# Low-rank feed-forward stage: the inner product in fp32r over split factors, and the order of the work around it

## The chip, the cores and the metric

One Trainium2 chip, one of its cores. The metric is the device time of one execution in microseconds; each version's number is the median of several executions. Smaller is better.

## What is computed

The reference is a network of eight stages over x (4 x 1024 rows of 256, fp32), in the order A M B M C F D F. Stages A and C are attentions, M is an expert feed-forward, B a retention, D a gated recurrence. This case is about F, which runs twice with the same weights, as stage 5 and as stage 7 (the last):

```python
def _L1_ffn_ref(x, U1, V1, b1, U2, V2, b2):
    D_MODEL, D_FF, RANK = (256, 1024, 64)
    P = jnp.einsum('bsd,dr->bsr', x, U1)
    H = jax.nn.gelu(jnp.einsum('bsr,rf->bsf', P, V1) + b1)
    Q = jnp.einsum('bsf,fr->bsr', H, U2)
    return jnp.einsum('bsr,rd->bsd', Q, V2) + b2
...
x = x + _L1_ffn_ref(_layernorm(x, axis=-1), L1_ffn_U1, ...)
```

So a row of 256 is normalised, brought down to 64 numbers, up to 1024 with a gelu, down to 64 and up to 256 again, and added to x.

## The kernel before, in words

X, all 4096 rows, stays in SBUF for the whole network. `low_rank_ffn` (L158) takes it in NG = 8 groups of 512 rows, each of them four tiles of 128. Every engine has its own program, in which the order of the work is written out by hand; the engines meet through semaphores that start at START = 4 and are waited for with constants or loop values.

What one group takes:

- **Row normalisation**, class `LayerNorm` (L70). VectorE takes four moments (L104, L107), GpSimd adds epsilon (L119) and raises to the power -1/2 (L123), VectorE scales the rows into `ln_h` (L113). There is one buffer of `ln_h`, so the rows of the next group wait until TensorE has transposed those of this one (L111). TensorE turns them over into `ps_t` (`tensor`, L125), ScalarE copies them to `hT` (`scalar`, L134).
- **first** (L273): U1 on the normalised rows. The 256 features are two halves; each half makes a product of 64 rows, the two of them side by side in the array's columns 0 to 63 and 64 to 127 (`tile_position`), so `ps_p` has two partial sums of P stacked on 128 partitions. ScalarE copies them to `PT` (L249).
- **hidden** (L281), the inner product: eight matmuls, m = 0 to 7, of V1 stacked twice (128 x 128) on `PT` (128 x 512) in fp32, which adds the two partial sums on the way. Their results go through two banks, `ps_h` (L179), to ScalarE's gelu (L255). The profile shows an fp32 matmul as two records.
- **down** (L286): U2, two matmuls of 64 columns side by side, into `ps_q`; ScalarE copies it to `QT` (L259).
- **out** (L311): V2 on `QT`, four matmuls of 256 columns into the two banks of `ps_o`; VectorE adds them to X (L239). GpSimd has added the bias b2 to the same rows of X before that (L223), once their normalisation was read.

The turns are skewed (`skewed_turns`, L147, a loop of three rounds with two turns each, and two turns behind it): in turn g the engines do the normalisation of group g + 2 besides. On VectorE it stands ahead of the two adds of group g (L234 to L240), on GpSimd ahead of the bias of group g (L219 to L224), on TensorE ahead of the last down. TensorE's order in a turn is: eight hidden matmuls with three downs between them, the transposes of g + 2, the last down, first of g + 1, and then the four of out, which wait for the copy `QT`.

The weights come in eight DMAs on SyncE's queue (L144). TensorE and ScalarE wait for all of them. The next stage begins when all engines have passed a barrier. In stage 7 SyncE also stores each group of X when its adds are done (L205).

Of the kernel before, what the change touches and what calls it, by code (L numbers as in the profile page):

```python
# [13 lines left out]
ds = bass.ds  # L14
# [143 lines left out]
def low_rank_ffn(nc, ph, X, ident, U1, V1, b1, U2, V2, b2, out=None):  # L158

    R, FF = U1.shape[1], V1.shape[1]
    M = FF // P
    hT = ph.sb("hT", [P, 2, DC, GT])
    u1 = ph.sb("u1", [P, DC, R])
    v1 = ph.sb("v1", [P, FF])  # L170
    bias1 = ph.sb("bias1", [P, M])
# [23 lines left out]
    with nc.Block() as block:  # L195
# [14 lines left out]
        def _(pool):  # L210
            ln.pool_setup()
            pool.wait_ge(ln.rs, START + 1)
            ln.pool(pool, 0)
            ln.pool(pool, 1)
            pool.wait_ge(weights, loaded)

            def turn(g, h, following, more):
                if more:
                    ln.pool(pool, g + 2)  # L219
                x4 = X[:, ds(g * G, G), :]  # L220
                pool.wait_ge(ln.hrow, START + (g + 1) * G)
                pool.sem_inc(passed, 1)
                nc.gpsimd.tensor_tensor(x4, x4, bias2[:, :].unsqueeze(1).to_broadcast([P, G, D]),  # L223
                                        ALU.add).then_inc(b_add, 1)  # L224
            skewed_turns(pool, turn)

        @block.vector
        def _(dve):
            ln.vector(dve, 0)
            ln.vector(dve, 1)  # L230

            def turn(g, h, following, more):
                if more:
                    ln.vector(dve, g + 2)  # L234
                dve.wait_ge(b_add, START + g + 1)
                for k in range(G // 2):
                    dve.wait_ge(o_mm, START + g * (G // 2) + k + 1)
                    x2 = X[:, ds(g * G + 2 * k, 2), :]
                    nc.vector.tensor_tensor(x2, ps_o[:, k, :].rearrange("p (j d) -> p j d", j=2), x2,  # L239
                                            ALU.add).then_inc(o_add, 1)  # L240
            skewed_turns(dve, turn)

        @block.scalar
        def _(act):
            act.wait_ge(weights, loaded)

            def first(g):
                act.wait_ge(p_mm, START + g + 1)
                nc.scalar.copy(PT[:, :], ps_p[:, :]).then_inc(p_sb, 1)  # L249

            def turn(g, h, following, more):
                act.wait_ge(q_mm, START + g)
                for m in range(M):
# [2062 lines left out]
```

## Time and profile before

| | us |
|---|---|
| median of 3 executions | 3752.79 (3745.21 to 3757.0) |
| the profiled execution, its own time | 3747.93 |
| its span, first to last instruction | 3746.0 |
| stage 7: weights landed to last add | 3610.35 to 3741.73 |

The profile is one execution. Engines: PE is TensorE's matmuls and PEld its weight loads, DVE is VectorE, ACT ScalarE, POOL GpSimd, SPq SyncE's queue. Times in a view are microseconds from the start of the span, except the mean of one instruction, which is in nanoseconds. Tiles carry the stage in their name: `s5F_` and `s7F_` are the two stages of this case. "<-" behind a tile name means made from; in square brackets stands how long the engine sat idle before, and what ended that. Granted clock 1.00 is TensorE at 2.4 GHz, 0.50 at 1.2 GHz.

### The profile page before, as it was taken

What the parts mean: (1) busy time and instruction counts of PE and PEld (TensorE: products, weight loads), DVE (VectorE), ACT (ScalarE), POOL (GpSimd) and SP (SyncE); (2) the same over time, 40 slices, a digit from 0 to 9 for tenths busy, and PEclk for the clock granted to TensorE, in tenths of its full rate; (3) what the DMA queues carried; (4) which work ended last, traced back from release to release, by engine and by line L of the source; (5) the groups of instructions that cost most, each with busy time, mean ns of one, the idle gap of its engine ahead of it and who ended that gap; (6) DMA issues with size and microseconds to landing.
All of it is one profiled execution on the core that took longest, in us unless ns stands there. A gap on an engine that the chain in (4) does not pass through costs nothing. (4 is left out here: it accounts for less than half of the span.)

```text
span 3746.0 us, 71603 instructions
## 1 busy us (share of the span) xinstructions
PE 3177.9 (85%) x21448; PEld 2163.5 (58%) x21448; DVE 2350.6 (63%) x5285; ACT 2075.7 (55%) x3467; POOL 854.2 (23%) x1660
## 2 busy tenths in 40 slices
PE   6699999999999639997883599959688888797879
PEld 3366666666666429996452499944355555533433
DVE  4488888888886564444557544435477777435853
ACT  3589898989897214443111344422267676354544
POOL 2211111111110114553001245523422222120112
PEclk9799999999999869998896799979899999898879
DMA  3300000000000314433003244331211111000001
GB/s 116 101 23 25 25 24 23 25 25 23 23 25 16 113 51 90 90 79 74 11 0 113 70 91 90 72 82 57 86 52 52 51 51 50 24 0 12 0 18 39
DMA packets 148660, 186.78 MB, mean 50 GB/s; under 512 B 20304, under 2 KB 114768, under 8 KB 148560
## 3 DMA queue, kind: packets, MB, share of 16 engines
q1 hardware_dynamic: 123984, 151.94, 12.6%
q0 software_dynamic: 24576, 33.57, 5.5%
q8 instruction: 55, 0.90, 0.1%
q14 instruction: 45, 0.37, 0.0%
HBM read 122.54 MB, written 62.91 MB: 50 GB/s over the span
## 5 line engine op out<-in xcount | busy, mean ns | idle before, releaser
L1741 DVE CUSTOM_DVE_ANT_0 s0Ah_SD<-s0Ah_ps_s,s0Ah_table 128x1024 f32<-128x1024 f32 x512 | 622.9, 1217 | 40.6 <-PE s0Ah_ps_s L1832 25.3
L1787 ACT ACTIVATE s0Ah_PM<-s0Ah_SD,s0Ah_nb 128x1024 f32<-128x1024 f32 x512 | 594.6, 1161 | 24.8 <-POOL s0Ah_nb L1730 24.8
L1842 PEld LDWEIGHTS s0Ah_ps_t<-top_ident,s0Ah_PM 128*128 128x128 f32 x4096 | 480.6, 141 | 103.1 <-ACT s0Ah_PM L1787 3.4
L1842 PE MATMUL s0Ah_ps_t<-top_ident,s0Ah_PM 128*128 128x128 f32 x4096 | 533.6, 273 | 0.4
L1793 ACT COPY s0Ah_PT<-s0Ah_ps_t 128x512 f32<-128x512 f32 x512 | 302.9, 592 | 104.3 <-PE s0Ah_ps_t L1842 99.8
L1832 PE MATMUL s0Ah_ps_s<-s0Ah_ks,s0Ah_qs 96*128 96x512 bf16 x1024 | 308.5, 383 | 28.4 <-DMA s0Ah_ks<-s0A_parts 27.7
L2045 ACT ACTIVATE s4Ch_PM<-s4Ch_SD,s4Ch_nb 128x260 f32<-128x260 f32 (+2 forms) x512 | 254.3, 497 | 141.1 <-POOL s4Ch_nb L1988 128.1
L1749 DVE COPY s0Ah_PT<-s0Ah_ps_t 128x512 f32<-128x512 f32 x384 | 264.8, 690 | 94.5 <-PE s0Ah_ps_t L1842 91.7
L1730 POOL TENSOR_TENSOR s0Ah_nb<-s0Ah_mx,s0Ah_minus 128x1 f32<-128x1 f32 x512 | 98.2, 192 | 930.8 <-DVE s0Ah_mx L1741 930.8
L1855 PE MATMUL s0Ah_ps_v<-s0Ah_PT,s0Ah_Vs 128*32 128x512 f32 x2048 | 274.2, 608 | 0.0
L1999 DVE CUSTOM_DVE_ANT_0 s4Ch_SD<-s4Ch_ps_s,s4Ch_table 128x260 f32<-128x260 f32 (+2 forms) x512 | 204.6, 407 | 78.9 <-PE s4Ch_ps_s L2090 65.5
L2090 PE MATMUL s4Ch_ps_s<-s4Ch_ks,s4Ch_qs 96*128 96x256 bf16 (+2 forms) x896 | 142.4, 229 | 111.8 <-DMA s4Ch_ks<-s4C_parts 55.9
L1832 PEld LDWEIGHTS s0Ah_ps_s<-s0Ah_ks,s0Ah_qs 96*128 96x128 bf16 x1024 | 82.2, 117 | 243.0 <-issue 239.9
L2108 PE MATMUL s4Ch_ps_t<-top_ident,s4Ch_PM 128*128 128x128 f32 x960 | 196.3, 281 | 0.0
L1988 POOL TENSOR_TENSOR s4Ch_nb<-s4Ch_mx,s4Ch_minus 128x1 f32<-128x1 f32 x512 | 98.0, 191 | 376.7 <-DVE s4Ch_mx L1999 376.6
L1193 ACT ACTIVATE s3Me_hid<-s3Me_ps_h 128x512 f32<-128x512 f32 x128 | 76.7, 599 | 184.3 <-PE s3Me_ps_h L1231 184.3
L1193 ACT ACTIVATE s1Me_hid<-s1Me_ps_h 128x512 f32<-128x512 f32 x128 | 76.7, 599 | 183.2 <-PE s1Me_ps_h L1231 183.2
L2090 PEld LDWEIGHTS s4Ch_ps_s<-s4Ch_ks,s4Ch_qs 96*128 96x128 bf16 x896 | 70.9, 98 | 171.6 <-DVE s4Ch_mx L1999 123.9
L2008 DVE COPY s4Ch_PT<-s4Ch_ps_t 128x512 f32<-128x512 f32 x192 | 132.6, 691 | 35.3 <-PE s4Ch_ps_t L2108 34.2
L1148 DVE TENSOR_TENSOR s3Me_HT_rest<-s3Me_hid,s3Me_HT_top 128x512 fp32r<-128x512 f32 x128 | 89.0, 695 | 103.7 <-ACT s3Me_HT_top L1194 103.7
L1148 DVE TENSOR_TENSOR s1Me_HT_rest<-s1Me_hid,s1Me_HT_top 128x512 fp32r<-128x512 f32 x128 | 88.9, 695 | 102.9 <-ACT s1Me_HT_top L1194 102.9
L1094 POOL DMA_INDIRECT s3M_acc<-s3Me_ys,s3Me_keep x64 | 109.6, 1712 | 167.7 <-DVE s3Me_ys L1158 153.1
(391 smaller groups left out, 7414.3 us busy)
## 6 DMA issues: line engine op xcount, KB each, us to landing
s1M_raw_w<-in_L_ffn_w SPq DMA_DIRECT2D x16, 1024.0 KB, 5.5
s3M_raw_w<-in_L_ffn_w SPq DMA_DIRECT2D x16, 1024.0 KB, 5.8
s0A_parts<-s0Ap_sp SPq DMA_DIRECT2D x48, 256.0 KB, 2.4
s4C_parts<-s4Cp_sp SPq DMA_DIRECT2D x48, 256.0 KB, 2.4
s0Ah_qs<-s0A_parts SPq DMA_DIRECT2D x64, 96.0 KB
s0Ah_ks<-s0A_parts SPq DMA_DIRECT2D x64, 96.0 KB
s4Ch_qs<-s4C_parts SPq DMA_DIRECT2D x64, 96.0 KB
s4Ch_ks<-s4C_parts SPq DMA_DIRECT2D x64, 96.0 KB
```

The costliest lines, as they stand in the source:

```text
L1148: nc.vector.tensor_tensor(HT[1][:, m, :], hid[:, m % NH, :], HT[0][:, m, :].bitcast(F32), ALU.subtract).then_inc(h_rest, 1)
L1741: nc.vector.tensor_tensor_reduce(SD[u % NBUF][:, :], ps_s[u % 2][:, :, :].rearrange("p a n -> p (a n)"), table[:, (TB - 1 - t) * P:(TB - 1 ...
L1749: nc.vector.tensor_copy(PT[u // G % 2][:, 0:G, q:q + P], ps_t[:, 0, :].rearrange("p (k q) -> p k q", k=G)).then_inc(ta_ok, 1)
L1787: nc.scalar.activation(PM[u % NBUF][:, :], SD[u % NBUF][:, :], ACT.Exp, bias=nb[:, u:u + 1]).then_inc(e_ok, 1)
L1793: nc.scalar.copy(PT[u // G % 2][:, G:, q:q + P], ps_t[:, 1, :].rearrange("p (k q) -> p k q", k=G)).then_inc(tb_ok, 1)
L1832: x = nc.tensor.matmul(ps_s[u % 2][:, k, :], qs[s][:, t * P:(t + 1) * P], ks[s][:, k * GT:(k + 1) * GT], start=True, stop=True)
L1842: x = nc.tensor.transpose(ps_t[:, bank, k * P:(k + 1) * P], PM[u % NBUF][:, at:at + P], ident[:, :])
L1855: x = nc.tensor.matmul(ps_v[j * W:(j + 1) * W, :], Vs[v // 2][:, 2 * j + r, :], PT[v % 2][:, 2 * j + r, :], start=(r == 0), stop=(r == 1), ...
L1999: nc.vector.tensor_tensor_reduce(SD[u % NBUF][:, 0:n], ps_s[u % 2][:, 0:n], table[:, min(u % TB, 2), 0:n], HD ** -0.5, -3e38, ALU.add, ALU ...
L2045: nc.scalar.activation(PM[u % NBUF][:, 0:n], SD[u % NBUF][:, 0:n], ACT.Exp, bias=nb[:, u:u + 1]).then_inc(e_ok, 1)
L2090: x = nc.tensor.matmul(ps_s[u % 2][:, at:at + n], qs[s][:, t * P:(t + 1) * P], ks[s][:, k0:k0 + n], start=True, stop=True)
L2108: x = nc.tensor.transpose(bank[:, u % 2, k if t else 1, :], pm[:, k * P:(k + 1) * P], ident[:, :])
```

## The change

- `u1` is loaded twice side by side (one DMA more), and `first` is two full matmuls that accumulate in `ps_p`, so P stands whole on partitions 0 to 63 and again on 64 to 127.
- P and V1 are split into a top, which is the value rounded to fp32r, and a rest, the difference. ScalarE makes `v1_top` once and VectorE `v1_rest` once per stage. Per group ScalarE makes `PA` (top of P, all 128 partitions) and the upper half of `PB` (top again), VectorE the lower half of `PB` (rest of P, `rest_of`).
- `hidden` takes two m at a time: two fp32r matmuls of 128 rows (`v1_top` on `PB`, top and rest stacked), and two of 64 rows (`v1_rest` on `PA`, one on partitions 0 to 63, the other on 64 to 127). The product of the two rests is left out. One semaphore step for both.
- `ps_h` has four banks instead of two, `ps_t` and `ps_o` one instead of two.
- Normalisation runs three groups ahead instead of two, with two buffers of `ln_h`. The transposes of a group are two separate steps (`turned`).
- The out matmuls of group g move into group g + 1 (`outs`), the adds of group g on VectorE likewise (`added`); VectorE's order in a group is: adds of g - 1, `rest_of(g + 1)`, normalisation of g + 3.
- The loops are unrolled. Two semaphores more.

Lines that the change takes out of the vector, scalar and tensor programs are left out below; they stand in the printed kernel.

```diff
@@ -157,36 +157,36 @@
 
 def low_rank_ffn(nc, ph, X, ident, U1, V1, b1, U2, V2, b2, out=None):
 
     R, FF = U1.shape[1], V1.shape[1]
     M = FF // P
+    NH = 4
     hT = ph.sb("hT", [P, 2, DC, GT])
-    u1 = ph.sb("u1", [P, DC, R])
+    u1 = ph.sb("u1", [P, DC, P])
     v1 = ph.sb("v1", [P, FF])
+    v1_top, v1_rest = ph.sb("v1_top", [P, FF], F32R), ph.sb("v1_rest", [P, FF], F32R)
     bias1 = ph.sb("bias1", [P, M])
     u2 = ph.sb("u2", [P, M, R])
     v2 = ph.sb("v2", [P, D])
     bias2 = ph.sb("bias2", [P, D])
-    PT, QT = ph.sb("PT", [P, GT]), ph.sb("QT", [P, GT])
+    PA = [ph.sb(f"PA{i}", [P, GT], F32R) for i in range(2)]
+    PB = [ph.sb(f"PB{i}", [P, GT], F32R) for i in range(2)]
+    QT = ph.sb("QT", [P, GT])
     HT = ph.sb("HT", [P, M, GT])
-    ps_t = ph.ps("ps_t", [P, DC, GT])
+    ps_t = ph.ps("ps_t", [P, GT])
     ps_p = ph.ps("ps_p", [P, GT])
-    ps_h = ph.ps("ps_h", [P, 2, GT])
+    ps_h = ph.ps("ps_h", [P, NH, GT])
     ps_q = ph.ps("ps_q", [P, GT])
-    ps_o = ph.ps("ps_o", [P, 2, GT])
-    ln = LayerNorm(ph, X, ident, hT, ps_t)
+    ps_o = ph.ps("ps_o", [P, GT])
+    ln = LayerNorm(ph, X, ident, hT, None, buffers=2)
     weights, stored = ph.dma_sem("weights"), ph.dma_sem("stored")
-    p_mm, p_sb = ph.sem("p_mm"), ph.sem("p_sb")
+    vt_ok, vr_ok = ph.sem("vt_ok"), ph.sem("vr_ok")
+    p_mm, top_ok, rest_ok = ph.sem("p_mm"), ph.sem("top_ok"), ph.sem("rest_ok")
     h_mm, h_sb = ph.sem("h_mm"), ph.sem("h_sb")
     q_mm, q_sb = ph.sem("q_mm"), ph.sem("q_sb")
-    b_add, passed = ph.sem("b_add"), ph.sem("passed")
+    b_add = ph.sem("b_add")
     o_mm, o_add = ph.sem("o_mm"), ph.sem("o_add")
-    pairs = [(u1[:, :, :], U1.rearrange("(c p) r -> p c r", p=P)), (v1[0:R, :], V1), (v1[R:P, :], V1),
+    split_u1 = U1.rearrange("(c p) r -> p c r", p=P)
+    pairs = [(u1[:, :, 0:R], split_u1), (u1[:, :, R:P], split_u1), (v1[0:R, :], V1), (v1[R:P, :], V1),
              (bias1[:, :], b1.rearrange("(m p) -> p m", p=P)),
              (u2[:, :, :], U2.rearrange("(m p) r -> p m r", p=P)), (v2[0:R, :], V2), (v2[R:P, :], V2),
              (bias2[:, :], b2.rearrange("(a d) -> a d", a=1).to_broadcast([P, D]))]
@@ -210,111 +210,167 @@
         def _(pool):
             ln.pool_setup()
             pool.wait_ge(ln.rs, START + 1)
-            ln.pool(pool, 0)
-            ln.pool(pool, 1)
+            for g in range(3):
+                ln.pool(pool, g, g % 2)
             pool.wait_ge(weights, loaded)
-            def turn(g, h, following, more):
-                if more:
-                    ln.pool(pool, g + 2)
-                x4 = X[:, ds(g * G, G), :]
+            for g in range(NG):
+                if g < NG - 3:
+                    ln.pool(pool, g + 3, (g + 3) % 2)
+                x4 = X[:, g * G:(g + 1) * G, :]
                 pool.wait_ge(ln.hrow, START + (g + 1) * G)
-                pool.sem_inc(passed, 1)
                 nc.gpsimd.tensor_tensor(x4, x4, bias2[:, :].unsqueeze(1).to_broadcast([P, G, D]),
                                         ALU.add).then_inc(b_add, 1)
-            skewed_turns(pool, turn)
 
         @block.vector
         def _(dve):
...
+            def rest_of(g):
+                dve.wait_ge(top_ok, START + 2 * g + 2)
+                nc.vector.tensor_tensor(PB[g % 2][R:P, :], ps_p[R:P, :], PA[g % 2][R:P, :].bitcast(F32),
+                                        ALU.subtract).then_inc(rest_ok, 1)
+
+            def added(g):
                 dve.wait_ge(b_add, START + g + 1)
                 for k in range(G // 2):
                     dve.wait_ge(o_mm, START + g * (G // 2) + k + 1)
...
+                    x2 = X[:, g * G + 2 * k:g * G + 2 * k + 2, :]
+                    nc.vector.tensor_tensor(x2, ps_o[:, :].rearrange("p (j d) -> p j d", j=2), x2,
                                             ALU.add).then_inc(o_add, 1)
...
+            def rows(g):
+                ln.vector_moments(dve, g, g % 2)
+                ln.vector_rows(dve, g, g % 2)
+            rows(0)
+            dve.wait_ge(vt_ok, START + 1)
+            nc.vector.tensor_tensor(v1_rest[:, :], v1[:, :], v1_top[:, :].bitcast(F32), ALU.subtract).then_inc(vr_ok, 1)
+            rows(1)
+            rest_of(0)
+            rows(2)
+            for g in range(NG):
+                if g:
+                    added(g - 1)
+                if g < NG - 1:
+                    rest_of(g + 1)
+                if g < NG - 3:
+                    rows(g + 3)
+            added(NG - 1)
 
         @block.scalar
         def _(act):
+            def turned(g, c):
+                act.wait_ge(ln.trans, START + g * DC + c + 1)
+                nc.scalar.copy(hT[:, g % 2, c, :], ps_t[:, :]).then_inc(ln.hTok, 1)
+
+            def tops(g):
+                act.wait_ge(p_mm, START + g + 1)
+                nc.scalar.copy(PA[g % 2][:, :], ps_p[:, :]).then_inc(top_ok, 1)
+                nc.scalar.copy(PB[g % 2][0:R, :], ps_p[0:R, :]).then_inc(top_ok, 1)
+
+            def hidden(g, m):
+                act.wait_ge(h_mm, START + g * (M // 2) + m // 2 + 1)
+                if m == 0:
+                    act.wait_ge(q_mm, START + g)
+                nc.scalar.activation(HT[:, m, :], ps_h[:, m % NH, :], ACT.Gelu_apprx_tanh,
+                                     bias=bias1[:, m:m + 1]).then_inc(h_sb, 1)
             act.wait_ge(weights, loaded)
...
+            nc.scalar.copy(v1_top[:, :], v1[:, :]).then_inc(vt_ok, 1)
+            for g in range(2):
+                for c in range(DC):
+                    turned(g, c)
+                if g == 0:
+                    tops(0)
+            for g in range(NG):
+                for m in range(4):
+                    hidden(g, m)
+                if g < NG - 2:
+                    turned(g + 2, 0)
+                for m in range(4, 6):
+                    hidden(g, m)
+                if g < NG - 1:
+                    tops(g + 1)
+                for m in range(6, 8):
+                    hidden(g, m)
+                if g < NG - 2:
+                    turned(g + 2, 1)
                 act.wait_ge(q_mm, START + g + 1)
                 act.wait_ge(o_mm, START + g * (G // 2))
                 nc.scalar.copy(QT[:, :], ps_q[:, :]).then_inc(q_sb, 1)
...
 
         @block.tensor
         def _(pe):
...
+            def turned(g, c):
+                if c == 0:
+                    pe.wait_ge(ln.hrow, START + (g + 1) * G)
+                pe.wait_ge(ln.hTok, START + g * DC + c)
+                for j in range(G):
+                    x = nc.tensor.transpose(ps_t[:, j * P:(j + 1) * P], ln.h[g % 2][:, j, c * P:(c + 1) * P], ident[:, :])
+                x.then_inc(ln.trans, 1)
+
+            def first(g):
                 pe.wait_ge(ln.hTok, START + (g + 1) * DC)
...
+                pe.wait_ge(top_ok, START + 2 * g)
+                pe.wait_ge(rest_ok, START + g)
+                for c in range(DC):
+                    x = nc.tensor.matmul(ps_p[:, :], u1[:, c, :], hT[:, g % 2, c, :], start=(c == 0), stop=(c == DC - 1))
+                x.then_inc(p_mm, 1)
 
             def hidden(g, m):
...
+                if m == 0:
+                    pe.wait_ge(rest_ok, START + g + 1)
+                pe.wait_ge(h_sb, START + g * M + m + 2 - NH)
+                for j in range(2):
+                    nc.tensor.matmul(ps_h[:, (m + j) % NH, :], v1_top[:, (m + j) * P:(m + j + 1) * P], PB[g % 2][:, :],
+                                     start=True, stop=False)
+                for j in range(2):
+                    half = slice(j * R, (j + 1) * R)
+                    x = nc.tensor.matmul(ps_h[:, (m + j) % NH, :], v1_rest[half, (m + j) * P:(m + j + 1) * P],
+                                         PA[g % 2][half, :], start=False, stop=True)
+                x.then_inc(h_mm, 1)
 
             def down(g, m):
+                if m == 0:
+                    pe.wait_ge(q_sb, START + g)
                 pe.wait_ge(h_sb, START + g * M + m + 2)
                 for j in range(2):
...
+                    x = nc.tensor.matmul(ps_q[j * R:(j + 1) * R, :], u2[:, m + j, :], HT[:, m + j, :],
                                          start=(m == 0), stop=(m == M - 2), tile_position=(0, j * R))
                 if m == M - 2:
...
+                    x.then_inc(q_mm, 1)
+
+            def outs(g, k):
+                n = g * (G // 2) + k
                 pe.wait_ge(q_sb, START + g + 1)
...
+                pe.wait_ge(o_add, START + n)
+                for j in range(2):
+                    at = (2 * k + j) * P
+                    x = nc.tensor.matmul(ps_o[:, j * D:(j + 1) * D], QT[:, at:at + P], v2[:, :], start=True, stop=True)
+                x.then_inc(o_mm, 1)
+            pe.wait_ge(weights, loaded)
+            turned(0, 0)
+            turned(0, 1)
+            first(0)
+            turned(1, 0)
+            turned(1, 1)
+            pe.wait_ge(vr_ok, START + 1)
+            for g in range(NG):
+                hidden(g, 0)
+                if g:
+                    outs(g - 1, 0)
+                hidden(g, 2)
+                if g:
+                    outs(g - 1, 1)
+                down(g, 0)
+                if g < NG - 2:
+                    turned(g + 2, 0)
+                hidden(g, 4)
+                down(g, 2)
+                if g < NG - 1:
+                    first(g + 1)
+                hidden(g, 6)
+                if g < NG - 2:
+                    turned(g + 2, 1)
+                down(g, 4)
+                down(g, 6)
+            outs(NG - 1, 0)
+            outs(NG - 1, 1)
 
 
 def retention(nc, ph, X, ident, a):
```

## Rows read from the trace of the kernel before

**Rows 1.** The page's first part: busy time and share of each engine.

```profile
PE 3177.9 (85%) x21448; PEld 2163.5 (58%) x21448; DVE 2350.6 (63%) x5285; ACT 2075.7 (55%) x3467; POOL 854.2 (23%) x1660
```

**Rows 2.** Windows, last stage, cut at group starts: length, busy times, granted clock, DMA.

```profile
3610.35:3618.64 8.29, 5.84 (x20) 3.44 (x21) 4.48 (x13) 3.14 (x6) 2.75 (x3) 0.50 0.01 2
3618.64:3635.90 17.26, 17.26 (x53) 7.02 (x54) 2.58 (x5) 8.72 (x13) 0.76 (x1) 0.90 0.00 0
3635.90:3651.25 15.35, 15.35 (x54) 6.09 (x53) 6.38 (x14) 8.00 (x13) 3.54 (x3) 1.00 0.10 34
...
sum 131.38, PE 127.51 PEld 50.94 DVE 44.41 ACT 65.42 POOL 25.95; mean PE 14.17 PEld 5.66 DVE 4.93 ACT 7.27 POOL 2.88
```

**Rows 3.** Chain that ended last, one group: start us, us, engine, tile, line.

```profile
3635.90 3.62 PE s7F_ps_h L283 x8
...
3640.53 1.92 PE s7F_ps_h L283 x4
3642.45 1.01 PE s7F_ps_q L290 x4
...
3646.38 1.02 PE s7F_ps_t L130 x8
...
3648.41 0.86 PE s7F_ps_p L277 x4
3649.27 1.98 PE s7F_ps_o L311 x8
```

**Rows 4.** Timeline of TensorE in the expert stage, fp32r, 512 columns.

```profile
1662.01 0.39 PE L1231 MATMUL s1Me_ps_h<-s1Me_xT_top,s1Me_w_top 128*128 128x512 f32 x1
1662.24 0.39 PE L1231 MATMUL s1Me_ps_h<-s1Me_xT_rest,s1Me_w_top 128*128 128x512 f32 x1
```

**Rows 5.** Timeline of VectorE and GpSimd in the same group: start us, us; idle before.

```profile
3636.67 1.40 DVE L104 BATCH_NORM_STATS2 s7F_ln_st<-top_X 128x6 f32 x4
...
3640.05 3.30 DVE L113 TENSOR_SCALAR s7F_ln_h<-top_X,s7F_ln_mv,s7F_ln_rstd 128x256 f32 x4 [1.52 <-POOL s7F_ln_rstd L123]
...
3638.88 1.02 POOL L123 TENSOR_TENSOR s7F_ln_rstd<-s7F_ln_ve,s7F_ln_mhalf 128x4 f32<-128x4 f32 x1
3639.87 2.35 POOL L223 TENSOR_TENSOR top_X<-top_X,s7F_bias 128x1024 f32 x1
```

**Rows 6.** Timeline of the last stage's start and end.

```profile
3604.19 1.38 DVE L113 TENSOR_SCALAR s7F_ln_h<-top_X,s7F_ln_mv,s7F_ln_rstd 128x256 f32<-128x256 f32 x4 [1.47 <-POOL s7F_ln_rstd L123]
3604.32 0.58 SPq L144 DMA_DIRECT2D s7F_u<-in_L_ffn_U  x1
...
3740.24 1.49 DVE L239 TENSOR_TENSOR top_X<-s7F_ps_o,top_X 128x512 f32<-128x512 f32 x2 [12.59 <-PE s7F_ps_o L311]
```

**Rows 7.** Groups by line: busy us, mean ns of one, idle before.

```profile
L255 ACT ACTIVATE s7F_HT<-s7F_ps_h,s7F_bias 128x512 f32<-128x512 f32 x64 | 44.0, 687 | 39.5 <-PE s7F_ps_h L283 39.0
L1182 ACT CAST s1Me_w_top<-s1M_raw_w 128x1024 fp32r<-128x1024 f32 x32 | 32.4, 1078 | 71.0 <-PEq L60 71.0
L1137 DVE TENSOR_TENSOR s1Me_w_rest<-s1M_raw_w,s1Me_w_top 128x1024 fp32r<-128x1024 f32 x32 | 37.8, 1223 | 2.4 <-ACT s1Me_w_top L1182 1.9
```

**Rows 8.** Timeline of ScalarE, two copies in a row.

```profile
3649.80 1.08 ACT L138 COPY s7F_hT<-s7F_ps_t 128x512 f32<-128x512 f32 x2
```

**Rows 9.** Waits of TensorE, 1815 to 1940 us; timeline rows behind two of stage D.

```profile
PE s2B_ps_t L130 <- DVE s2B_ln_h L113: 12.9, 6, 2.2
...
3497.00 6.43 PE L736 MATMUL s6D_ps_f<-s6D_hT,s6D_wf 128*128 x8 [3.48 <-DVE top_X L664]
...
3519.20 1.70 PE L736 MATMUL s6D_ps_f<-s6D_hT,s6D_wf 128*128 x2 [2.78 <-DVE top_X L664]
```

**Rows 10.** Windows of 5 us from the end of ten such gaps; the clock is third last.

```profile
1822.63:1827.63 5.00, 5.00 (x20) 4.31 (x21) 0.33 (x1) 1.17 (x2) 0.00 (x0) 0.66 0.00 0
...
1868.81:1873.81 5.00, 5.00 (x26) 4.35 (x27) 0.98 (x2) 1.07 (x2) 0.00 (x0) 1.00 0.00 0
...
3564.02:3569.02 5.00, 5.00 (x8) 2.23 (x9) 4.37 (x7) 2.02 (x7) 0.00 (x0) 0.66 0.00 0
```

More of the change, by code:

```diff
@@ L243, in _ @@
         @block.scalar
         def _(act):
-            act.wait_ge(weights, loaded)
[L247 to L253, printed above, removed]
-                    act.wait_ge(h_mm, START + g * M + m + 1)
-                    nc.scalar.activation(HT[:, m, :], ps_h[:, m % 2, :], ACT.Gelu_apprx_tanh,
-                                         bias=bias1[:, m:m + 1]).then_inc(h_sb, 1)
+            def turned(g, c):
+                act.wait_ge(ln.trans, START + g * DC + c + 1)
+                nc.scalar.copy(hT[:, g % 2, c, :], ps_t[:, :]).then_inc(ln.hTok, 1)
@@ L259, in turn @@
                 nc.scalar.copy(QT[:, :], ps_q[:, :]).then_inc(q_sb, 1)
-                if following:
-                    first(g + 1)
-                if more:
-                    ln.scalar(act, g + 2, h)
-            ln.scalar(act, 0, 0)
-            ln.scalar(act, 1, 1)
-            first(0)
-            skewed_turns(act, turn)
         @block.tensor
         def _(pe):
-            pe.wait_ge(weights, loaded)
-            def first(g, h):
+            def turned(g, c):
[5 more added lines that the diff above has]
+                x.then_inc(ln.trans, 1)
@@ L281, in hidden @@
             def hidden(g, m):
-                pe.wait_ge(h_sb, START + g * M + m - 1)
-                nc.tensor.matmul(ps_h[:, m % 2, :], v1[:, m * P:(m + 1) * P], PT[:, :],
-                                 start=True, stop=True).then_inc(h_mm, 1)
+                if m == 0:
[4 more added lines that the diff above has]
+                                     start=True, stop=False)
@@ L286, in down @@
+                for j in range(2):
[3 more added lines that the diff above has]
+                x.then_inc(h_mm, 1)
             def down(g, m):
+                if m == 0:
+                    pe.wait_ge(q_sb, START + g)
                 pe.wait_ge(h_sb, START + g * M + m + 2)
                 for j in range(2):
-                    i = nc.tensor.matmul(ps_q[j * R:(j + 1) * R, :], u2[:, m + j, :], HT[:, m + j, :],
+                    x = nc.tensor.matmul(ps_q[j * R:(j + 1) * R, :], u2[:, m + j, :], HT[:, m + j, :],
@@ L291, in down @@
                                          start=(m == 0), stop=(m == M - 2), tile_position=(0, j * R))
                 if m == M - 2:
-                    i.then_inc(q_mm, 1)
-            def turn(g, h, following, more):
-                pe.wait_ge(p_sb, START + g + 1)
-                pe.wait_ge(q_sb, START + g)
-                for m in range(M):
-                    hidden(g, m)
-                    if m >= 3 and m % 2:
-                        down(g, m - 3)
-                if more:
-                    ln.tensor(pe, g + 2)
-                down(g, M - 2)
-                if following:
-                    first(g + 1, 1 - h)
-                pe.wait_ge(q_sb, START + g + 1)
-                pe.wait_ge(o_add, START + g * (G // 2))
-                for k in range(G // 2):
-                    for j in (2 * k, 2 * k + 1):
-                        i = nc.tensor.matmul(ps_o[:, k, (j % 2) * D:(j % 2 + 1) * D], QT[:, j * P:(j + 1) * P],
-                                             v2[:, :], start=True, stop=True)
-                    i.then_inc(o_mm, 1)
@@ L314, in _ @@
-            ln.tensor(pe, 0)
-            ln.tensor(pe, 1)
-            first(0, 0)
-            skewed_turns(pe, turn)
+                    x.then_inc(q_mm, 1)
+            def outs(g, k):
+                n = g * (G // 2) + k
+                pe.wait_ge(q_sb, START + g + 1)
+                pe.wait_ge(o_add, START + n)
[3 more added lines that the diff above has]
+                x.then_inc(o_mm, 1)
```

12 lines of the change are left out of this document (removed).

## The prediction

> **What bounds the kernel now.** I read the page first: TensorE is busy 85% of the span, the others much less [rows 1]. That is an average over eight stages, so I cut stage 7 into windows at the starts of its groups [rows 2]. From the landing of the weights to the last add it takes 131.38 us: 8.29 before the first hidden matmul, a first group of 17.26 at a mean clock of 0.90, groups of 15.35, a last one of 14.81. In a middle group TensorE is busy for all of 15.35 us at clock 1.00; VectorE has 6.38 and ScalarE 8.00. TensorE is the bound, and the chain of waits agrees: within a group it is all PE [rows 3]. Stage 5 is the same code with the same weights, so I count each change twice.
>
> The chain gives prices at full clock: a pair of hidden m 1.92, a pair of down 1.01, eight transposes 1.02, first 0.86, out 1.98 [rows 3]. The first hidden four of a group take 3.62, so hidden costs 3.62 + 2 x 1.92 = 7.46, down 4 x 1.01 = 4.04, and 7.46 + 4.04 + 1.02 + 0.86 + 1.98 = 15.36, the window.
>
> **TensorE's own work after the change.** An fp32r matmul of 512 columns starts 0.23 us after the one before it [rows 4]; an fp32 record takes 0.43 (1.92 for four, less about 0.2 for the change of tiling). A pair of m is now two fp32r matmuls, 0.46, and two of 64 rows. Those are nowhere in this trace as fp32r in two halves of the array. Bounds: side by side, as the two halves of down run, 0.23; one behind the other, 0.46. I take side by side, since down's pair (1.01 for four records) is the nearest row. A change between whole and tiled costs 0.1 to 0.15 each way by the same rows (down 1.01 against 2 x 0.43), so a pair is 0.46 + 0.23 + 0.25 = **0.95**, at most 1.2. Hidden falls from 7.46 to 3.8. First grows: two full fp32 matmuls, four records one behind the other, 1.7 + 0.1 = 1.8, up 0.95. Out is 2 x 0.96. The sum: 3.8 + 4.0 + 1.0 + 1.8 + 1.9 = 12.5 of work. If TensorE stayed the bound, each group would gain nearly 3 us.
>
> **What is late instead.** I followed the new waits. `ps_o` has one bank, so the second `outs(g, 1)` waits for the first add of `added(g)`. That add is in VectorE's program behind `rows(g + 3)`, and that behind `rest_of(g + 1)`, which waits for `tops(g + 1)`, which waits for `first(g + 1)`. And `first(g + 2)` is behind `outs(g, 1)` on TensorE. This is a closed loop, once round per group. Its parts:
>
> - `rest_of`: as long as an add of 512 columns out of PSUM, 0.69 [rows 6], 0.6 net of overlap.
> - Normalisation of g + 3, from the first moment at 3636.67 to the last row at 3643.35: 6.67 us [rows 5]. It is that long because the scaling takes 3.30 beside GpSimd's bias of 2.35, and 1.38 without it [rows 6]. In the new order GpSimd still raises to the power and then adds a bias at once, so both meet again. Before, this lay under TensorE's work at no cost.
> - The first add, 0.69 (half of 1.49 with its handover) [rows 6], and 0.1 of semaphore: 0.7. So far 8.0.
> - TensorE: out 0.96, down 1.01, four transposes 0.5, hidden 0.95, down 1.01, first to its last result 2.0 (a record's result comes 0.16 behind its slot, 0.39 against 0.23 [rows 4]): 6.4.
> - ScalarE: two copies, 1.08 [rows 8], and 0.1 of handover: 1.2.
>
> 8.0 + 6.4 + 1.2 = **15.6 us per round**, against 15.35 before. TensorE has 12.5 of work in it and stands for some 3 us ahead of `outs(g, 1)`. Normalisation runs five more times in the loop (g = 0 to 4), so five groups cost 15.6. The one behind them and the last have no such wait.
>
> **The sum for a stage**, from the landing of the weights. One more DMA issue (0.58 [rows 6]) and two semaphores: +0.7. Start: ScalarE first makes `v1_top`, 1.08 [rows 7], then the transposes, with one bank, alternate with their copies: 1.1 + 0.6 + 1.0 + 0.6; first at half clock takes 3.4, the two tops 1.1, the copy and transposes of group 1 another 1.6: the first hidden at 9.7 instead of 8.29. `v1_rest`, 1.22 on VectorE, is under that. Group 0, with a clock as low as before for its first part, 13.8 (it has no outs). Five of 15.6: 78.2. Group 6, 12.2. The last 14.7: its hidden part is shorter, but the tail is copy 0.6, out 1.0, add 0.8, out 1.0, add 0.8 in turn, because of the one bank. 0.7 + 9.7 + 13.8 + 78.2 + 12.2 + 14.7 = 129.3, which is 2 less than 131.4; some 4 us less for two stages.
>
> Free edits: four banks of `ps_h` and the single step for a pair (ScalarE is ahead of down in all but the last pair, gelus at 687 ns [rows 7]; without that cover some 0.4 per group); unrolling (a table load of 1.28 less per two groups on ScalarE, under TensorE); the bias stays under TensorE except through the loop above.
>
> **The clock.** TensorE never stood still in a middle group; now it stands 3 us in each of five. What happens then can be read elsewhere in this trace. In stage B it waits six times 2.1 to 2.2 us for the rows; in stage D four times 2.8 to 3.5 us for an add [rows 9] (and twice longer, which I leave out). In the 5 us behind those ten gaps the mean clock was 0.66 six times, 0.50 once, 1.00 three times [rows 10]: so after seven of ten gaps the engine fell from 2.4 to 1.2 GHz for 3.4 us or more. What follows this gap is the part of the loop on TensorE, all of it on the path. 3.4 us at half clock cost 1.7; 0.7 x 1.7 = 1.2 per gap, 6 per stage, 12 for ten gaps. Bounds: none, 0; always twice as long, 34.
>
> The Trainium skill has a rule that speaks against this change ("TensorE: Matmul & The Clock Gate", section "A second HAM failure mode: psum-queue depth-cycling"): a TensorE that stands briefly between groups of matmuls while it cycles through PSUM banks can be throttled and released again and again, though its clock looks right at the median. By it alone all ten gaps would cost, which is rival C; the ten gaps of this trace say seven in ten.
>
> **Forecast (A).** -4 + 12 = +8 us. The profiled execution took 3747.93, 4.9 below the median of the runs; I put the difference on the median, 3752.79 + 8 = about **3760**. The measurement can tell some 0.3% from no change, 11 us, so this is no change that can be told, leaning to slower.
>
> **Rivals.**
> - **B, TensorE stays the bound**: the loop doesn't close, since normalisation is short (1.38 instead of 3.30) and waits overlap more than I think. 12.5 and about 0.5 of stalls is 13.0 per group: six groups of 2.35 less, 14 to 15 per stage, -29: 3724. With only the scaling short the round is 13.6, 2 x 5 x 2 less than A without clock losses: 3729. For it: the loop is made of small parts. Against it: 3.30 was taken in the same order of GpSimd's instructions.
> - **C, slower by the clock**: place, behind `outs(g, 1)`; price 1.7 per 3.4 us at 1.2 GHz. It decides from 15 us on, that is, from nine of ten gaps, or from fewer where it stays low for 6.8 (once in seven above). All ten short: -4 + 17 = +13, 3766; all long: +30, 3783.
> - **D, the 64-row halves don't run side by side**: 0.25 on one pair in the loop, ten rounds: +2.5, inside A; in B 1 us per group, so half of B's gain would stay.
>
> **Chances.** A 0.50, within 0.3%. B 0.22, faster. C, with the upper end of A, 0.28, slower. Range: B's 3724 to C's 3783 are the ends; I leave out a little of each, 3726 to 3781. A's own range is 3749 (no clock loss) to 3764.
>
> **What would show it.** In the after windows: groups 1 to 5 of 15.6 (17 where the clock fell), TensorE busy some 12.5 to 13 of them; a wait of TensorE at `ps_o` for VectorE's add, x5 per stage, about 3 us each; a hidden pair of 0.95; the first two rows at L113 beside the bias still over 3 us; the clock under 1.00 in the middle groups. Group 6 near 12.2 shows TensorE's own work. Windows of 13 throughout and no such wait would prove me wrong (B), as would a `ps_o` wait that is shorter than 1 us.

## The result, and the profile after

The change took the median from 3749.78 us (five executions, 3745.21 to 3757.0) to **3770.84 us** (five, 3765.63 to 3784.37): a ratio of 1.0062, 95% interval 1.0038 to 1.0085. That is slower by 0.6%. The forecast was 3760, no change that can be told and leaning to slower, with slower as its second case; 3770.84 lies in the range. The forecast was its +8 on 3752.79, the median of the three executions known then; on 3749.78 the same +8 gives 3758.

The profiled execution of after is the longest of its five, 3784.37, with a span of 3782.4. Its stage 4, whose code is not touched, took 753.9 us, from its first instruction to its last matmul, against 742.9 in the profile of before, and in the profiles of the ten kernels below, which leave it alone too, it took anything from 734.9 (e6) to 755.3 (e7). So I read windows of stages 5 and 7, and not the two spans. The page's first part, after, answers to [rows 1]:

```profile
PE 3167.0 (84%) x21448; PEld 2169.9 (57%) x21448; DVE 2366.2 (63%) x5303; ACT 2071.2 (55%) x3481; POOL 850.4 (22%) x1660
```

TensorE is busy for 11 us less on the page, and the program is longer. By windows it is some 20 us less in stages 5 and 7 (127.46 to 117.85 and 127.51 to 116.93), as the change meant it to be, and more in the longer stage 4. The windows of stage 7, cut at group starts as in [rows 2] (length, then busy time of PE, PEld, DVE, ACT and POOL, granted clock, DMA share, GB/s):

```profile
3634.97:3644.38 9.41, 7.04 (x21) 3.78 (x21) 5.19 (x15) 3.73 (x6) 1.20 (x2) 0.60 0.00 1
3644.38:3656.77 12.39, 11.04 (x47) 4.30 (x45) 5.07 (x17) 8.82 (x14) 1.21 (x2) 1.00 0.01 1
3656.77:3674.38 17.61, 14.61 (x54) 6.22 (x52) 7.27 (x15) 7.65 (x13) 3.53 (x3) 0.90 0.09 30
...
3691.76:3710.52 18.76, 15.80 (x55) 6.99 (x53) 7.27 (x15) 7.65 (x13) 3.54 (x3) 0.82 0.09 29
3710.52:3728.03 17.51, 14.55 (x55) 6.39 (x53) 7.27 (x15) 7.65 (x13) 3.54 (x3) 0.90 0.09 30
3728.03:3749.62 21.59, 14.58 (x55) 6.33 (x53) 9.92 (x11) 7.65 (x13) 10.59 (x6) 0.84 0.08 25
3749.62:3762.23 12.61, 12.16 (x47) 4.92 (x45) 2.08 (x3) 6.59 (x11) 0.00 (x0) 1.00 0.12 42
...
sum 142.78, PE 116.93 PEld 50.76 DVE 54.11 ACT 63.63 POOL 27.16; mean PE 12.99 PEld 5.64 DVE 6.01 ACT 7.07 POOL 3.02
```

The stage went from 131.38 to 142.78. Groups 1 to 4 take 17.4 to 18.8 us instead of 15.35, and group 5, the window from 3728.03, takes 21.59. In each TensorE stands for about 3 us or more, and the clock is below 1.00. Group 6, without that wait, is 12.61. Stage 5 went from 131.3 to 143.8 in the same pattern. With the weights landing 0.8 us later in each stage the two stages are 25.5 us longer in this pair of profiles; the medians, which also hold stage 4, differ by 21.

Where TensorE stands is in the view of waits (waiting tile and line, releaser: us in all, count, longest):

```profile
PE s5F_ps_o L344 <- DVE top_X L236: 19.9, 6, 7.0
PE s7F_ps_o L344 <- DVE top_X L236: 19.8, 6, 7.0
```

Five of the six are the gaps of groups 1 to 5, 18.9 us together in stage 7; the sixth, 0.94, is at the stage's end. There was no such wait before. The timeline of VectorE, GpSimd and TensorE around the first and around the fifth of these waits (start us, us, instruction, in brackets the idle time before):

```profile
3658.57 2.36 POOL L221 TENSOR_TENSOR top_X<-top_X,s7F_bias 128x1024 f32<-128x1024 f32 x1
3658.64 3.41 DVE L113 TENSOR_SCALAR s7F_ln_h<-top_X,s7F_ln_mv,s7F_ln_rstd 128x256 f32<-128x256 f32 x4 [1.46 <-POOL s7F_ln_rstd L123]
...
3662.07 0.69 DVE L236 TENSOR_TENSOR top_X<-s7F_ps_o,top_X 128x512 f32<-128x512 f32 x1
...
3662.91 1.93 PE L344 MATMUL s7F_ps_o<-s7F_v,s7F_QT 128*128 128x256 f32 x4 [3.00 <-DVE top_X L236]
...
3729.77 7.05 POOL L221 TENSOR_TENSOR top_X<-top_X,s7F_bias 128x1024 f32<-128x1024 f32 x3
3729.84 7.46 DVE L113 TENSOR_SCALAR s7F_ln_h<-top_X,s7F_ln_mv,s7F_ln_rstd 128x256 f32<-128x256 f32 x4 [1.41 <-POOL s7F_ln_rstd L123]
...
3738.16 2.04 PE L344 MATMUL s7F_ps_o<-s7F_v,s7F_QT 128*128 128x256 f32 x4 [7.01 <-DVE top_X L236]
```

The scaling of the rows (L113), 1.38 us alone [rows 6], takes 3.41 beside one bias of GpSimd and **7.46** beside three. Three run in a row here because the biases are in order behind the normalisations: the bias of group 4 comes after the power of group 7, the last, and 5 and 6 then wait for nothing. The add behind the scaling comes late by that, and TensorE waits 3.00 and 7.01 us.

The Trainium skill ("SBUF — State Buffer", section "Who interferes with whom") says that VectorE and GpSimd share a pair of ports as an exclusive lock: while VectorE runs in a mode that uses both of its ports, whoever issues first has the pair for its whole instruction, and the other is blocked, not slowed. The rows agree. The four scalings that make up the 7.46, one by one (ns, shortest, median and longest):

```profile
L113 DVE TENSOR_SCALAR s7F_ln_h<-top_X,s7F_ln_mv,s7F_ln_rstd x4: 401/2424/2443, 3729.8 to 3736.9; 128x256 f32<-128x256 f32 x4
```

Three of them take 2.43 us each. They start 0.06 to 0.12 us behind the start of a bias of 2.36 to 2.39 and end 0.15 us behind its end; the fourth, after the last bias, takes 0.40. So it is one scaling for each bias. Which of VectorE's modes they run in, no view shows.

### The profile page after: what moved, and what is told of

The parts are those of the page before. It is cut to its first block and busy times, and to the rows that moved or that the text cites. A ratio compares the mean times of both kernels' runs of the same rounds, so it can differ in the third digit from the quotient of the medians.

```text
span 3782.4 us, 71181 instructions
## 1 busy us (share of the span) xinstructions
PE 3167.0 (84%) x21448; PEld 2169.9 (57%) x21448; DVE 2366.2 (63%) x5303; ACT 2071.2 (55%) x3481; POOL 850.4 (22%) x1660
## 5 line engine op out<-in xcount | busy, mean ns | idle before, releaser
L1150 POOL DMA_INDIRECT s1M_acc<-s1Me_ys,s1Me_keep x64 | 111.3, 1740 | 164.8 <-DVE s1Me_ys L1214 150.2
```

## The experiments

Theory L: a closed loop over VectorE and TensorE sets the round and its gap brings the clock down (both from the prediction), and three biases in a row beside the scaling lengthen one gap per stage (read only from the profile after). The main rivals: the new inner product is itself the slow part; or the gap costs little and the clock falls for another reason.

**1. The fifth gap.** `e3_last_biases_late` lets the biases of groups 5 to 7 wait until all rows are normalised.

```diff
-                pool.wait_ge(ln.hrow, START + (g + 1) * G)
+                pool.wait_ge(ln.hrow, START + (g + 1 if g < NG - 3 else NG) * G)
```

> The changed kernel, but the biases of groups 5, 6 and 7 wait until the last scaling is done, so one bias instead of three runs beside it. Theory: the fifth gap of TensorE falls from 7.0 to 3.0 us, the other four stay, 4 us less per stage, about 3763. Rival (the fifth gap is long because the clock was low there): it stays near 7, 3771.

3765.9 us, 1.0045 of before (1.0029 to 1.0062). Group 5 in the windows, and its scaling in the timeline:

```profile
3713.84:3731.35 17.51, 14.54 (x54) 6.39 (x52) 5.87 (x11) 7.66 (x13) 10.54 (x6) 0.90 0.09 31
```

```profile
3715.65 3.42 DVE L113 TENSOR_SCALAR s7F_ln_h<-top_X,s7F_ln_mv,s7F_ln_rstd 128x256 f32<-128x256 f32 x4 [1.41 <-POOL s7F_ln_rstd L123]
```

21.59 became 17.51: the three biases cost 4.1 us per stage, and no other group of stage 7 moved. This rests on the windows: the medians of e3 and after are 4.9 us apart, and the intervals of their ratios overlap.

**2. The clock.** `e4_gap_filled` keeps TensorE at work in the gap with matmuls whose results nothing reads (three fp32 ones, seven in group 5). What TensorE waits for there, VectorE's add, stays the same.

```diff
+                if 0 < g < NG - 2:
+                    pe.wait_ge(ln.hTok, START + (g + 2) * DC)
+                    for _ in range(3 if g < NG - 3 else 7):
+                        nc.tensor.matmul(ps_t[:, :], ident[:, :], v1[:, 0:GT], start=True, stop=True)
                 if g:
                     outs(g - 1, 1)
```

> The changed kernel with work added that nobody reads: where TensorE would stand ahead of the second outs, it multiplies the identity with 512 columns of V1 into the free ps_t, three fp32 matmuls (2.6 us) in groups 1 to 4 and seven (6.0 us) in group 5. Theory: the loop is the same, so at full clock a round is 15.7; the gap is 0.4 instead of 3.0 us and the clock stays at 1.00, so the 1.7 us and more per round that the low clock costs come back: 9 us less per stage, about 3752, although TensorE does more. Rival (the clock falls for another reason than the gap, such as the 64-row halves): granted clock below 1.00 as before and 3771 or more.

3751.71 us, 1.0017 (1.0002 to 1.0033). The windows of groups 1 and 5:

```profile
3629.81:3645.80 15.99, 15.71 (x60) 6.79 (x58) 7.29 (x15) 7.65 (x13) 3.54 (x3) 1.00 0.09 33
...
3693.62:3713.64 20.02, 19.15 (x69) 8.31 (x67) 9.95 (x11) 7.65 (x13) 10.63 (x6) 1.00 0.08 26
```

Useless work made the stage 9.0 us shorter, 142.78 to 133.76, since the clock stays at 1.00. This measures two things: the gaps bring the clock down and that costs 9 us per stage; and the round without it is 15.95, a little longer than the old group. The add is still what ends the wait (0.28 us of it are left ahead of `outs` at 3635.97), so 15.95 is the loop's length and not that of the added work. The two medians are 19 us apart, of the 21 lost.

**3. Breaking the loop in two places.** `e1_rows_first` has VectorE do the normalisation of g + 3 ahead of `rest_of(g + 1)`, under time in which it would wait for `tops`. `e2_bias_early` has GpSimd add the bias of g before it takes up g + 3, so that scaling and bias don't meet; this leaves the loop closed and makes it shorter. `e7_both_orders` has both.

VectorE, in e1 and e7:

```diff
-                if g < NG - 1:
-                    rest_of(g + 1)
                 if g < NG - 3:
                     rows(g + 3)
+                if g < NG - 1:
+                    rest_of(g + 1)
```

GpSimd, in e2 and e7:

```diff
-                if g < NG - 3:
-                    ln.pool(pool, g + 3, (g + 3) % 2)
...
-                pool.wait_ge(ln.hrow, START + (g + 1) * G)
+                pool.wait_ge(ln.hrow, START + min(g + 3, NG) * G)
...
+                if g < NG - 3:
+                    ln.pool(pool, g + 3, (g + 3) % 2)
```

> The changed kernel with one exchange on VectorE: in each group rows(g + 3) stands ahead of rest_of(g + 1) instead of behind it. Theory (closed loop): the round tops, rest_of, rows, added, outs is cut, because rows no longer waits for the tops. TensorE's own work is then the bound: middle groups of 12.5 to 13.5 us instead of 17.5, no wait of TensorE for VectorE's add over 1 us, clock 1.00 in the middle groups. 28 us less per stage than the changed kernel, about 3715. Rival (the new matmuls themselves are slow: halves, changes of tiling): middle groups stay above 15 us and the time above 3750. Second rival (scaling beside three biases in the end): the first four middle groups fall, the fifth stays 4 us longer, 3723.

> The changed kernel with GpSimd's order changed alone: the bias of group g is added right behind the scaling of group g + 2 and ahead of GpSimd's part of group g + 3, so that no bias runs beside a scaling. Theory: the loop stays, but the scaling takes 1.4 instead of 3.4 (and instead of 7.4 in the fifth), so the round is 13.7 to 14, the gap ahead of the second outs about 1 us, and the fifth gap of 7.0 is gone with it. The clock falls seldom or not. 22 to 24 us less per stage, about 3725. Rival (the scaling is long for another reason, such as the second buffer): no change, 3771.

> The changed kernel with both exchanges, rows(g + 3) ahead of rest_of(g + 1) on VectorE and the bias behind the scaling of g + 2 on GpSimd. Theory: all five middle groups are TensorE's 13.0 us, also the fifth and sixth (16.5 and 15.4 to 15.7 with the first exchange alone), clock 1.00 throughout the middle; about 115 us per stage, 3715, a gain of 0.9% on the kernel before. Rival (VectorE becomes the bound, since rest_of now waits for the scaling): groups above 13.5 and a wait of TensorE for rest_of.

e1 took 3728.79, 0.9942 (0.9922 to 0.9961): 14 us above the first number expected for it. Its groups 1 to 3 are 13.01, as expected, but then come 16.45 and 15.44. The timeline shows why:

```profile
3671.13 7.09 POOL L221 TENSOR_TENSOR top_X<-top_X,s7F_bias 128x1024 f32<-128x1024 f32 x3
...
3671.20 7.50 DVE L113 TENSOR_SCALAR s7F_ln_h<-top_X,s7F_ln_mv,s7F_ln_rstd 128x256 f32<-128x256 f32 x4 [1.41 <-POOL s7F_ln_rstd L123]
3678.73 0.69 DVE L228 TENSOR_TENSOR s7F_PB<-s7F_ps_p,s7F_PA 64x512 fp32r<-64x512 f32 x1
...
3679.47 1.22 PE L320 MATMUL s7F_ps_h<-s7F_PB,s7F_v_top 128*128 128x512 f32 x2 [3.38 <-DVE s7F_PB L228]
```

The three biases hold up the scaling again, and in this order it is `rest_of` that is behind it: one wait of 3.38 us, and 6.8 us at 1.2 GHz. The second rival of the expectation (3723) had named these three biases; it put them in the fifth group and left out the clock behind them.

e2 took 3724.32, 0.9946 (0.9928 to 0.9963), as expected. Its gap:

```profile
PE s7F_ps_o L344 <- DVE top_X L236: 5.6, 6, 0.9
```

Five groups of 13.90, and the clock at 1.00 for 112.6 us: the five stops of 0.94 us in these groups did not bring it down, those of 3.0 did each time.

e7 took **3714.36**, 0.9901 (0.9884 to 0.9918), one per cent faster than before and the lowest median of those that compute the same. Its middle groups:

```profile
3640.70:3653.71 13.01, 12.95 (x55) 5.74 (x53) 5.15 (x15) 7.65 (x13) 3.60 (x3) 1.00 0.12 40
```

TensorE is busy 12.95 of 13.01: this is its own work per group after the change, which the prediction had put at 12.5, and at 13.0 with stalls. Beside 15.35 the whole change is worth 2.34 us per group once nothing is in its way. Of that 0.46 is the new order's and 1.88 the new product's, since the new order with the old product (e5, below) has groups of 14.89.

**4. The parts alone.** `e5_new_order_old_product` keeps the new order of the work, buffers and queues, and puts the old fp32 product back (V1 stacked on partial sums, no `rest_of`). `e6_old_order_new_product` is the kernel before with the fp32r product, one m at a time because it has two banks.

The matmuls of e5 against after, and of e6 against before:

```diff
-                    nc.tensor.matmul(ps_h[:, (m + j) % NH, :], v1_top[:, (m + j) * P:(m + j + 1) * P], PB[g % 2][:, :],
-                                     start=True, stop=False)
-                for j in range(2):
...
+                    x = nc.tensor.matmul(ps_h[:, (m + j) % NH, :], v1[:, (m + j) * P:(m + j + 1) * P], PT[g % 2][:, :],
+                                         start=True, stop=True)
```

```diff
-                nc.tensor.matmul(ps_h[:, m % 2, :], v1[:, m * P:(m + 1) * P], PT[:, :],
-                                 start=True, stop=True).then_inc(h_mm, 1)
+                half = slice(m % 2 * R, (m % 2 + 1) * R)
+                nc.tensor.matmul(ps_h[:, m % 2, :], v1_top[:, m * P:(m + 1) * P], PB[:, :], start=True, stop=False)
+                nc.tensor.matmul(ps_h[:, m % 2, :], v1_rest[half, m * P:(m + 1) * P], PA[half, :],
+                                 start=False, stop=True).then_inc(h_mm, 1)
```

> The new order of work, banks and buffers with the old fp32 inner product (stacked partial sums, one copy to PT, no tops, no rest_of, V1 not split). Theory: without rest_of the normalisation of g + 3 waits for nothing of TensorE but the adds of g - 1, so the loop is open; TensorE is the bound with its old work, 15.3 to 15.6 us per group, clock 1.00, no wait for VectorE's add over 1 us. About the time of the kernel before, 3748 to 3757, the end a little longer because of the one bank of ps_o. Rival (the order alone, through the one bank of ps_o, costs the time): gaps of 3 us as in the changed kernel, above 3765.

> The old order, banks and loop with the new inner product: first as two full matmuls, tops and rest, one m at a time (one fp32r matmul of 128 rows, one of 64 rows), two banks of ps_h. Theory: there is no closed loop through the normalisation, since rest_of stands behind it and the adds need only the outs of the same turn; but with two banks each m waits for the gelu two before it, and the hidden part starts only after first, tops and rest. 15.0 to 15.8 us per group, about 3752, so the new product without the new order gains little or nothing. Rival (the fp32r product alone is what makes it slow): 17 us per group and above 3765. Other rival (it alone is a gain): below 3735.

e5 took 3749.5, 1.0006 (0.9991 to 1.0021), as expected: the normalisation waits for no `rest_of`, so the loop is open, TensorE is busy for all of 14.89 us in each middle group, and the clock stays at 1.00. In the sum the new order alone is worth nothing and costs nothing. Its parts are not nothing: a middle group is 14.89 instead of 15.35, group 0, which has no outs now, 14.73 instead of 17.26, and the last one, which has those of two groups and ends in outs and adds that take turns over one bank, 18.31 instead of 14.81. The stage is 130.23 us instead of 131.38.

e6 was expected near 3752 and took **3807.97**, 1.0165 (1.014 to 1.0189). Theory L did not see this. Even its groups at full clock are 15.90, longer than the old ones, and the others are 20 to 24 us. Windows of e6, cut where the clock changed:

```profile
3640.70:3657.70 17.00, 17.00 (x33) 6.05 (x33) 4.02 (x10) 5.50 (x8) 3.53 (x3) 0.50 0.01 1
3657.72:3681.60 23.88, 23.02 (x78) 10.47 (x76) 10.44 (x24) 13.27 (x21) 3.56 (x3) 1.00 0.09 31
3681.60:3698.70 17.10, 17.10 (x35) 5.65 (x35) 3.52 (x8) 4.12 (x6) 3.54 (x3) 0.50 0.06 19
```

For some 17 us at a time the engine is at 1.2 GHz although it is busy for all of them, and in the 24 us before the second fall its longest stop was 0.33 us. (Ahead of the first of these stretches stood a stop of 2.06 us, at the start of the stage.) Stage 5 has two such falls without a stop over 0.33 us, each for 13.65 us. So a long stop is not the only thing that goes ahead of a fall. What e6 has and no other kernel here has is a stream in which a 128-row fp32r matmul and a 64-row one take turns, one by one. Their timeline at full clock:

```profile
3664.77 0.50 PE L297 MATMUL s7F_ps_h<-s7F_PB,s7F_v_top 128*128 128x512 f32 x1
3665.20 0.49 PE L298 MATMUL s7F_ps_h<-s7F_PA,s7F_v_rest 64*128 64x512 f32 x1
3665.63 0.49 PE L297 MATMUL s7F_ps_h<-s7F_PB,s7F_v_top 128*128 128x512 f32 x1
```

Each starts 0.43 us after the one before, against 0.23 between two of one shape [rows 4]: the change of shape costs 0.2 each time (the same two matmuls over 128 rows, in e9 below, start 0.23 apart: 3652.11, 3652.34, 3652.57), and an m costs 0.86, little less than the 0.96 of fp32.

`e9_old_order_whole_array` is e6 with the second matmul over all 128 rows: V1's rest is halved (one more VectorE instruction per stage) and both halves, which hold the same, are summed.

```diff
-                nc.tensor.matmul(ps_h[:, m % 2, :], v1_rest[half, m * P:(m + 1) * P], PA[half, :],
+                nc.tensor.matmul(ps_h[:, m % 2, :], v1_rest[:, m * P:(m + 1) * P], PA[:, :],
```

> The old order with the new product once more (3808 before, every second group 22.2 us at a clock of 0.50 although TensorE never stood longer than 0.33 us in a middle group), but the rest product of each m is one fp32r matmul of all 128 rows: V1's rest, halved, stacked twice, on the two copies of P's top. Theory: what let the clock fall there was the stream of single 64-row matmuls, each with a change of tiling, in which half the array does nothing; with the whole array in each matmul the clock stays at 1.00, hidden falls from 0.85 to 0.5 to 0.7 per m (then the gelu paces it), groups of 14 to 15.9 throughout, 3735 to 3760. Rival (the short stops of 0.2 to 0.3 us for gelus let it fall): there are more of them now, so low stretches as before and above 3780.

3741.76, 0.9992 (0.998 to 1.0005), as expected. The stage is 129.42 instead of 171.91, and most groups stay at 1.00:

```profile
3647.45:3662.03 14.58, 13.47 (x53) 6.46 (x53) 6.92 (x16) 8.89 (x15) 3.57 (x3) 1.00 0.11 36
...
3690.70:3708.15 17.45, 15.12 (x53) 7.09 (x53) 8.96 (x16) 7.61 (x14) 8.29 (x5) 0.90 0.09 31
```

Here TensorE stands still for more of the time than in e6, 1.1 us of 14.58, with stops up to 0.87, and the clock holds for 78.5 us; behind the start of the stage it falls only after a stop of 1.86 us (group 5, where two biases run beside the scaling). The two kernels differ in whether half of the array lies idle in every second matmul, and in the change of shape that goes with it; which of the two brings the clock down is open. Nor does the stream of e6 bring it down every time: in stage 5 the clock stayed at 1.00 for the last 50 us.

**5. TensorE's own work.** `e8_no_rest_of_V1` is e7 without the two 64-row matmuls of a pair: V1's rounding error is left out. `e10_both_orders_whole_array` is e7 with them over all 128 rows, as in e9.

> As both exchanges together, but the two 64-row matmuls of each pair are left out, so the product of V1's rest with P is missing from the output. It prices them where TensorE is the bound. Side by side with the change of tiling: 0.4 to 0.5 us per pair, 1.7 to 2.1 per group, about 14 per stage, 3688. One behind the other they would cost 0.7 or more per pair, 2.8 per group, 3670 or less. If ScalarE (8.4 us busy of 11) or VectorE takes over as the bound, less than 1.5 per group comes back.

> Both exchanges together (3714), and the rest product of each m as one fp32r matmul of all 128 rows (V1's rest, halved, on both copies of P's top), so a pair has four matmuls of 0.23 and no change of tiling inside it, against 0.66 + 0.43 now. Theory (TensorE is the bound): 0.1 to 0.15 us less per pair, groups of 12.4 to 12.6 instead of 13.0, about 8 us less in all, 3706. Rival (two matmuls more per pair cost more than the change of tiling they save): groups above 13.0 and 3714 or more.

e8 took 3710.11, 0.9888 (0.9871 to 0.9906): groups of 12.23 instead of 13.01, a gain of 0.78, where the halves side by side were expected to give 1.7 to 2.1 and one behind the other 2.8. The third case named, less than 1.5 if another engine becomes the bound, is what came. TensorE waits again:

```profile
3656.51 1.10 PE L340 MATMUL s7F_ps_o<-s7F_v,s7F_QT 128*128 128x256 f32 x4 [0.48 <-DVE top_X L236]
...
3664.91 1.08 PE L329 MATMUL s7F_ps_q<-s7F_HT,s7F_u 128*64 128x512 f32 x4 [0.39 <-ACT s7F_HT L271]
```

Half of what was taken away had covered VectorE's add and ScalarE's gelu. TensorE's busy time did fall, 12.95 to 11.34 us, 1.6 per group.

e10 took 3719.85, 0.9922 (0.9904 to 0.994), with groups of 12.88: the whole array gains 0.13 us per group, not the 0.4 to 0.6 expected, and in the medians it can't be told from e7. Two 64-row halves side by side with their changes of shape (a pair of m is 1.09 us) cost nearly what two 128-row matmuls cost (1.04). The halves do run at once. In the trace of after the two of a pair start within 0.01 us of each other (3728.69), and the groups by line say the same: 64 of them, 503 ns each, in 16.2 us of busy time, half of 64 x 0.503.

```profile
L324 PE MATMUL s7F_ps_h<-s7F_PA,s7F_v_rest 64*128 64x512 f32 x64 | 16.2, 503 | 0.0
```

## Why the prediction was right where it was, and wrong where it was

**The loop** was right, and so was its place: a wait at `ps_o` for VectorE's add, some 3 us, five times per stage. Its length at full clock is 15.95 (e4) instead of 15.6. By its own parts: `rest_of` and normalisation 7.46 instead of 7.3 (in after, from `rest_of` at 3654.59 to the end of the scaling at 3662.05), add and handover 0.86 instead of 0.7 (to 3662.91), TensorE 6.5 instead of 6.4 (in e4, at full clock), ScalarE 1.13 instead of 1.2. Five rounds: +1.8 us per stage.

**The hidden pair** was mis-sized: 1.09 instead of 0.95. The side-by-side halves were right (rival D is false), the changes of shape take 0.40 in a pair and not 0.25. In the loop this is part of the 0.35; it also puts group 6 at 12.61 instead of 12.2.

**The fifth gap** is the step that was missing. "Normalisation of g + 3, from the first moment ... 6.67 us" was taken for all five rounds. In the fifth GpSimd has no further normalisation and three biases run in a row: +4.1 us per stage, shown by e3. The prediction took the round of the first four for the fifth without walking GpSimd's program to its end. It could have been read before: the timeline of VectorE in the last group with a normalisation had the same thing with two biases, hidden under TensorE:

```profile
3701.53 5.33 DVE L113 TENSOR_SCALAR s7F_ln_h<-top_X,s7F_ln_mv,s7F_ln_rstd 128x256 f32 x4 [1.52 <-POOL s7F_ln_rstd L123]
```

**The clock** had the right sign and mechanism, and too low a rate. The prediction took "after seven of ten gaps" 3.4 us at half clock, 6 us per stage. The clock fell behind ten of ten, four of them for 6.8 us or more, and it cost 9.0 (e4): +3.0 per stage. What the other stages' gaps told was too mild for these. Six of the ten were of 2.1 to 2.2 us, and the two of stage D that the prediction left out for being longer, 5.7 and 4.5 us, have 6.8 us at 1.2 GHz behind each in the same trace (3471.82 to 3478.64 and 3540.09 to 3546.91). The rule of the Trainium skill that the prediction weighed ("TensorE: Matmul & The Clock Gate", section "A second HAM failure mode: psum-queue depth-cycling") agrees with the ten of ten; it speaks of an engine that idles between groups of matmuls, and e6 shows the clock fall behind stretches whose longest stop is 0.33 us.

**Start and end**: the first hidden at 9.41 (9.7 forecast), group 0 at 12.39 (13.8; its clock was at 1.00 throughout), the last group 15.52 (14.7).

Added up against the forecast's sum: +1.8 + 4.1 + 3.0 in the five rounds, less 0.2 that they had in rounding, and -0.3 - 1.4 + 0.4 + 0.8 around them, make 8.2 us per stage. The forecast was 134.6 with its clock losses, the window is 142.78. The two stages give 16, and +8 becomes +24; the medians show +21. So half of the miss is the fifth gap, which none of the cases had priced. That 3770.84 still lies in the range is in part luck: the range reaches up to 3783 because C let the clock stay low for longer, and that room held the biases too.

Of the rivals, **B** was false as a forecast and true as a potential: 13.0 us per group is what e7 reaches once the loop is opened. **C** names what happened, slower by the clock, and its point of decision held: all ten gaps, some of them long. A had been put ahead of it, 0.50 to 0.28, because three of ten foreign gaps had stayed without a cost; here A, no change that can be told, did not come true.

## What to carry to other kernels

When a change takes work off the engine that bounds, list what that work was covering, and price each wait with the neighbour engines as they will run then: the same scaling cost 1.4, 3.4 or 7.5 us by what GpSimd did beside it, and here the order of two lines on VectorE and of two on GpSimd decided between 0.6% slower and 1.0% faster. Walk the last rounds of a skewed loop separately, since the engine that runs out of look-ahead work does its leftovers all at once. A gap of TensorE costs its length and the clock behind it. Here the clock took 9.0 of the 11.4 us that stage 7 lost, and matmuls that nothing reads, put into the gaps, gave them back (e4).

## What the runs showed of the hardware that was not expected

- TensorE at 1.2 GHz for 17.1 us (3681.60 to 3698.70) while it was busy for all of them, with no stop over 0.33 us in the 24 us ahead (e6), and at 2.4 GHz with stops up to 0.87 us once every matmul used all 128 rows (e9).
- A change between 128-row and 64-row fp32r matmuls costs 0.2 us per matmul where they alternate (0.43 instead of 0.23 from start to start), so that half the rows bought nothing.
- VectorE's four scalings, 1.38 us alone, take 7.46 beside three GpSimd additions in a row: three of the four take 2.43 each, one beside each addition, and the last ends 0.5 us after the last addition.
- Stops of 3 to 7 us brought the clock down ten times of ten (after). Shorter ones give no clean order: those of 1.86 and 1.88 us did (e9, stages 7 and 5), the one of 2.41 us in group 0 of both stages of e8 did not, nor did the 0.94 us of e2's middle groups; but at the end of e2's stage 5 the clock fell behind two stops in a row, of 0.69 and 0.94 us (3375.34 and 3377.15; the fall is at 3378.22).
